# Softmax scaling of the selected-block attention moved from VectorE to GpSimd

## The reference

```python
# compressed branch: 225 overlapping 4x4 blocks, each turned into one key and one value by an MLP
attn_cmp = softmax(einsum('bhnd,bhmd->bhnm', q_c, kch) * SCALE)          # 4 heads, 1024 x 225
# selected branch: the 16 blocks with the largest summed attn_cmp, 16 tokens each = 256 keys
_, idx = top_k(attn_cmp.sum(axis=1).mean(axis=1), 16)
attn_slc = softmax(einsum('bhnd,bhmd->bhnm', q_s, ksh) * SCALE)          # 4 heads, 1024 x 256
out_slc = einsum('bhnm,bhmd->bhnd', attn_slc, vsh) @ proj_slc_w + proj_slc_b
# window branch: 25 windows of 7x7 with a relative bias
out = g[0] * out_cmp + g[1] * out_slc + g[2] * out_win
x = x + out
# then, per token: layer norm, router, layer norm, 2 of 8 experts (gelu MLP 128 -> 512 -> 128)
```

## Time and profile before

| | |
|---|---|
| median of 3 executions | 891.06 us (890.48 to 892.27) |
| span of the profiled execution | 921.8 us |
| TensorE busy | 716.2 us, 78% |
| VectorE busy | 593.9 us, 64% |
| ScalarE busy | 414.4 us, 45% |
| GpSimd busy | 240.6 us, 26% |
| first and last scaling (L897) | at 76.8 and 678.7 us |
| mean granted TensorE clock | 0.890 |

### The profile page before, as it was taken

How to read it: one execution, slowest core, us unless ns; L and a number is a source line. 1 busy time by engine, 2 the same in 40 slices (tenths; PEclk the granted TensorE clock), 3 DMA queues, 4 the chain that set the end, 5 groups by cost and what they waited for, 6 DMA issues and landing times.

```text
span 921.8 us, 18341 instructions
## 1 busy us (share of the span) xinstructions
PE 716.2 (78%) x4992; PEld 534.2 (58%) x4993; DVE 593.9 (64%) x1930; ACT 414.4 (45%) x1203; POOL 240.6 (26%) x399
## 2 busy tenths in 40 slices
PE   3998778799578788976778799577873089999963
PEld 2794444679244455964444588244452079999962
DVE  4647858788377778856869787477767234444434
ACT  2227327324353453326427333453531158887852
POOL 5000220210604002124220210604001635555540
PEclk9999969899888799989979999978885589999995
DMA  9600000000100000000000000101002212222236
GB/s 324 194 1 0 4 3 0 25 23 1 48 1 4 1 23 1 24 20 29 3 3 0 2 24 1 47 1 28 1 1 114 70 49 64 69 63 64 62 93 235
DMA packets 34225, 39.66 MB, mean 43 GB/s; under 512 B 11246, under 2 KB 26720, under 8 KB 33888
## 3 DMA queue, kind: packets, MB, share of 16 engines
q1 hardware_dynamic: 28592, 27.73, 9.9%
q0 software_dynamic: 4416, 9.00, 2.9%
q10 hardware_dynamic: 1152, 2.10, 0.6%
HBM read 25.38 MB, written 14.50 MB: 43 GB/s over the span
## 4 chain that ended last, share of the span: by engine, by line
PE 44%; issue 24%; DVE 18%; POOL 4%; DMA 3%; ACT 2%; another core or an unknown queue 2%; POOLq 1%; SPq 1%; DVEq 0%; ACTq 0%
PE ps L1579 7%; PE ps L1563 7%; PE ps L1330 6%; PE ps L1479 6%; PE ps L1353 4%; PE ps L1278 3%; PE ps L1321 2%; DVE r_P L897 2%; DVE r_kp L1096 2%; PE ps L1297 2%; PE ps L1272 2%; DVE nmx L887 2%; POOL xs_d L607 2%; DMA kbdw<-z_d 1%
## 5 line engine op out<-in xcount | busy, mean ns | idle before, releaser
L1353 PE MATMUL ps<-kbd,qT 128*128 128x450 f32 (+1 forms) x256 | 131.6, 653 | 16.2 <-issue 15.1
L668 ACT ACTIVATE r_P<-ps,nmx 128x225 f32<-128x225 f32 (+1 forms) x192 | 85.8, 461 | 91.1 <-DVE nmx L887 90.5
L887 DVE TENSOR_REDUCE nmx<-ps 128x4 f32<-128x900 f32 (+1 forms) x64 | 74.0, 1157 | 80.4 <-PE ps L1353 61.1
L804 ACT ACTIVATE R<-ps,R 128x128 f32<-128x128 f32 x292 | 83.3, 368 | 46.0 <-PE ps L1563 44.7
L1353 PEld LDWEIGHTS ps<-kbd,qT 128*128 128x128 f32 x256 | 52.2, 221 | 69.1 <-issue 66.8
L607 POOL DMA_INDIRECT xs_d<-pay,pos x64 | 62.2, 972 | 102.9 <-DVE pos L1077 84.6
L643 POOL DMA_INDIRECT z_d<-R x72 | 69.4, 964 | 67.3 <-DVE R L1243 53.2
L552 POOL TENSOR_TENSOR rstd<-vpe,minus_half 128x8 f32<-128x8 f32 x12 | 19.8, 1651 | 251.9 <-DVE vpe L862 251.9
L1272 PE MATMUL ps<-ident,r_P 128*128 128x128 f32 (+1 forms) x384 | 57.7, 297 | 34.8 <-DVE r_P L897 22.2
L1272 PEld LDWEIGHTS ps<-ident,r_P 128*128 128x128 f32 (+1 forms) x384 | 47.1, 157 | 60.1 <-DVE r_P L897 35.7
L1563 PE MATMUL ps<-R 128*128 128x128 f32 x584 | 79.3, 280 | 0.0
(11 more groups left out here) (208 smaller groups left out, 1388.2 us busy)
## 6 DMA issues: line engine op xcount, KB each, us to landing
R<-xs_d SPq DMA_DIRECT2D x76, 65.0 KB
kbdw<-z_d SPq DMA_DIRECT2D x8, 512.0 KB, 5.5
x_sb<-x SPq DMA_DIRECT2D x4, 512.0 KB, 3.5
w1k_sb<-w1k SPq DMA_DIRECT2D x1, 2048.0 KB, 10.2
w1v_sb<-w1v SPq DMA_DIRECT2D x1, 2048.0 KB, 14.6
fw_sb<-fw SPq DMA_DIRECT2D x1, 2048.0 KB, 10.5
fw_sb<-fw SPq DMA_DIRECT2D x4, 512.0 KB, 11.0
t_d<-r_P SPq DMA_DIRECT2D x4, 512.0 KB, 2.6
```

Of the source, the lines that this page charges most:

```text
L668: last = sc.activation(Pb[t % NRING][:, h, 0:m], bank(ph, name)[:, (h % 2) * m:(h % 2) * m + m], ACT.Exp, bias=nmx[:, t % NRING, h:h + 1], ...
L804: last = sc.activation(hT[:, r % 2, c, :], hid(r)[:, C * c:C * c + C], ACT.Gelu, bias=wx[:, r, O_B1 + c:O_B1 + c + 1])
L887: ve.tensor_reduce(nmx[:, t % NRING, :].rearrange("p (a h) -> p a h", a=2), v.rearrange("p a (h m) -> p a h m", h=2), AX.X, ALU.max, negat ...
L1353: mm(bank(ph, name)[:, 0:2 * mk], qT[:, 128 * t:128 * t + 128], kbd[:, 2 * k:2 * k + 2, 0:mk], start=True, stop=True).then_inc(full_sem(ph ...
```

## The change

In the selected branch (`s == "s"`) VectorE only makes the reciprocals and signals `rz_ready`. The scaling is made on GpSimd by a new function, `scale_selected`, which issues one product of 128 x 1024 elements for each tile, with the four reciprocals of a token broadcast over 256 keys each, and then signals `prob_ready`. It stands behind `windows(b)` and ahead of `head` in GpSimd's program. The wait for `dve_done` between reciprocal and scaling falls away in this branch (8 links fewer for an image). The compressed branch stays as it is.

```diff
-    LINKS_FIRST, LINKS_MIDDLE = 7, 67
+    LINKS_FIRST, LINKS_MIDDLE = 7, 59
...
+        rz_ready = sem("rz_ready")
...
+            def scale_selected(b):
+
+                for t in range(NT):
+                    pool.wait_ge(rz_ready, b * NT + t + 1)
+                    v = Pb[t % NRING][:, :, 0:256]
+                    gp.tensor_tensor(v, v, rZ[:, t % NRING, :].unsqueeze(2).to_broadcast([128, HEADS, 256]),
+                                     ALU.mult).then_inc(prob_ready, 1)
...
                 windows(b)
+                scale_selected(b)
                 head(middle_one(b), b + 1, 3 * b + 1)
...
             windows(B - 1)
+            scale_selected(B - 1)
...
                     dve.wait_ge(*copied(ph, f"S{s}{t}b"))
+                    if s == "s":
+                        ve.reciprocal(rZ[:, t % NRING, :], Z[:, t % NRING, :]).then_inc(rz_ready, 1)
+                        return
                     link(ve.reciprocal(rZ[:, t % NRING, :], Z[:, t % NRING, :]))
```

## The result

The changed kernel takes 898.55 us (median of 4 runs, 898.04 to 899.08), the kernel before, timed beside it, 890.93 us (890.48 to 892.27). By the medians it is 7.6 us slower, where +8.8 us was forecast. The ratio is 1.0069 with a 95% interval of 1.0041 to 1.0097, which is 6.1 us (3.7 to 8.6); it isn't the quotient of the two medians (1.0086), but its interval holds that too.

What follows compares the result with a forecast made beforehand. VectorE was taken to bound the selected stage at 2.98 us a tile; the longer latency loop then adds 2.2 us an image, 4 x 2.2 = +8.8 us on 891.06, giving 899.9 us, range 891 to 907 us.

Steps and rivals of the forecast that it cites:

- What bounds before: First stage of the selected branch: VectorE sets the pace, 2.98 us a tile; the latency loop's 2.73 us is hidden.
- The product: GpSimd's scaling product of 128 x 1024: 1.925 us, from a line through two other shapes.
- The loop: Latency loop over two tiles in the selected stage, through the scaling: 5.45 us becomes 6.29, 3.15 us a tile.
- the prediction's formula: TensorE's transposes in the selected stage: each of two turns from T(0) to T(4) takes 4.37 + d us.
- The walk: Event by event through the first selected stage: T(0) 0.84 us later, T(4) 2.0, the stage's end 2.2.
- The rival of the relief: Selected stage: taking scalings off VectorE wins if the product is short; -1.0 us an image, 887 us, chance 0.09.
- lower bound: GpSimd's product at the copy's rate, 1.05 us: T(4) 0.6 us earlier, -1.0 us for an image.
- The sum: Selected stage 2.2 us longer in each of four images: +8.8 us, from 891.06 to 899.9 us.
- the rival priced at up to 1 us an image: Selected stage: product takes 2.20 us (904.7 us), or more TensorE idling lowers the clock (909 us); chance 0.15.
- Hidden: The selected stage's delay is swallowed, or unprofiled runs have another critical step: 890 to 893 us, chance 0.07.
- What is free: GpSimd's eight waits in the selected stage delay nothing in its queue, and no DMA is added.
- The carried difference: The median of the runs lies 30.7 us below the profiled span of 921.8 us; carried over unchanged.

Runs made afterwards that it cites:

- e12: Kernel before with one more step between scores and transposes in the selected branch and O0 moved to step 7; 909.47 us, ratio 0.9892.
- e2: Changed kernel, but GpSimd scales heads 0 and 1, VectorE heads 2 and 3 in the plain form; TensorE waits for both; 907.64 us, ratio 1.0208.
- e3: Changed kernel, but GpSimd scales three heads and VectorE one in the plain form; TensorE waits for both; 910.66 us, ratio 1.0206.
- e4_half_left_out: Changed kernel with GpSimd scaling only heads 0 and 1, heads 2 and 3 left unscaled; 882.48 us, ratio 0.9893.
- e11_three_heads_accum: Same as e3, but VectorE scales its one head in the form that also writes a sum; 924.47 us, ratio 1.0040.
- e1: Changed kernel without any scaling in the selected branch; VectorE's reciprocal releases TensorE directly; 876.95 us, ratio 0.9820.
- e5: Changed kernel with one more step between scores and transposes in the selected branch and a fourth buffer of probabilities; 911.24 us, ratio 1.0194.
- before again: Kernel before, unchanged, run for a second profile of an ordinary execution; median 891.98 us, ratio 0.9997.
- first profile: Profiled execution of the kernel before, unchanged, that the prediction read; span 921.8 us.
- e7: Same as e2, but VectorE scales its two heads in the form that also writes a sum; 889.11 us, ratio 0.9955.
- The last four kernels: Four follow-up kernels: three with an extra step and O0 moved to step 7, one the three-head split in summing form; 908.44 to 924.47 us.

## Why the prediction was right

**What bounds before.** Confirmed: with a fourth tile in flight and VectorE's scalings kept (e12) the distance stays at 2.99 us; VectorE was the bound and not the loop.

**The product.** 1.892 us for 1.925 (x32, 1892 to 1894 ns). The line through two other shapes was right to 2%. With the products of e2 and e3 it is 1039, 1466 and 1892 ns for 512, 768 and 1024 elements: 1.67 ns an element and 0.19 us fixed. A piece of 256 elements is hardly cheaper than one of 49 (1.67 against 1.714 ns an element). That is 2.0 cycles at 1.2 GHz; the Trainium skill's figure of about 2.6, "GPSIMD Engine Reference", section 3.1, is above it, and the rows were the better source.

**The loop.** By the prediction's formula two turns, T(0) to T(4), take 2 x (4.37 + d) for a product of d us:

| product us | kernel | formula | measured |
|---|---|---|---|
| 1.041 | e4_half_left_out | 10.82 | 10.81 |
| 1.468 | e11_three_heads_accum | 11.68 | 11.66 |
| 1.892 | changed kernel | 12.52 | 12.50 |

The slope is that of latency: each microsecond on the product is one on the turn. The line ends just below e4. Without any product (e1, image 2) T(0) to T(4) still takes 10.83 us, since its first turn takes 5.65; its second, T(2) to T(4), takes 5.18 us, TensorE's own pace, against 5.40 in e4, 5.83 in e11 and 6.25 in the changed kernel, where the formula says 5.41, 5.84 and 6.26. The middle of e5 is the other side of the proof: the same product, only the step added, and no delay once a third tile spans the turn. VectorE's scalings that stand explain e2 and e3 but not the changed kernel, where VectorE has no scaling beside the product.

**The walk.** In image 2 the shifts are 0.80, 1.60, 1.87 and 2.13 us where 0.84, 1.7, 2.0 and 2.2 were forecast; nearly all of the rest is the 0.03 us that the product is shorter, up to four times over. In the first stage, where the walk was made, it is 0.53 us at T(0) and 1.55 at O1's start. One step was misread there: the walk lets T(7) start at 163.44 before the change, behind the last scaling, but T(6) ran at the low clock until then and the first matmul of T(7), the ninth of the 16 in that row, starts at 163.82 in that trace. The walk's own shift for that stage would have been 1.8 us.

The rival of the relief was priced right only up to T(7). With e4's product of 1.04 us T(4) comes 0.69 us earlier and T(7) 1.05 in image 2, where its lower bound said 0.6 and 1.0. But it made that 4 us in all, 887 us, and e4 is 9.3 us faster: its stages are 2.6 us shorter an image, since T(7) and O1 take 1.09 and 1.93 us there, against 1.59 and 2.69 in "before again".

**The sum.** +8.8 us became +7.6 by the medians, +6.1 by the ratio. Up to O1's start it is +8.6, by image 1.55, 3.17, 1.64, 2.25. Image 1 is above 2.2 because T(0) is already 1.60 us later there: the scores ahead of it took 8.32 us where they take 6.77 in "before again". The term that was off is the one I set to nothing in the forecast: the clock at the end of the stage. It acts already ahead of O1. T(7) in image 2, in "before again" and then in the changed kernel (us, busy times, and the granted clock as the third number from the end):

```profile
490.00:492.00 2.00, 1.59 (x8) 1.19 (x8) 1.27 (x2) 0.77 (x2) 0.00 (x0) 0.64 0.00 0
```
```profile
496.00:498.00 2.00, 1.31 (x16) 0.99 (x20) 0.69 (x1) 0.99 (x2) 0.00 (x0) 1.00 0.00 0
```

T(7) takes 1.59 us at 0.64 and 1.09 at 1.00, so the 2.13 us at its start are 1.64 at O1's. In "before again" O1 takes 1.93, 2.72, 2.69 and 3.64 us in the four images, after the change 3.64 in image 0 (granted clock 0.51, second window above), 2.47 in image 1 and 1.93 in images 2 and 3. What the rival priced at up to 1 us an image, more idle time ahead of T(6) and T(7), can be seen in image 0: O1 takes 1.7 us more there. In the other three it takes 0.3, 0.8 and 1.7 us less, and over the four 1.0 us comes back. Nothing here forecasts where the low stretches fall, so I call this part luck.

**Hidden.** Fell: no wait swallowed a part of the delay. Where less arrives at O1's start than at T(7)'s, in image 2, it is T(7)'s own clock. **What is free.** The compressed branch takes 122.5 us in sum in both kernels, and the stretch between the branches 122.8 and 122.5.

**The carried difference.** The 30.7 us between span and median had nothing to do with the stage, whose sum is 126.8 us in that first profile and 126.7 in "before again". In the first profile the compressed branch took 29.3, 39.5, 36.3 and 42.1 us in the four images, in "before again" 29.3, 30.0, 30.6 and 32.5.

## What to carry to other kernels

Before moving work off a busy engine, write down the loop that passes through the moved step: its latency over the number of tiles it spans is the pace that is left when the engine is free, and here (4.37 + 1.89)/2 = 3.13 us was more than the engine's 2.98. If the loop is the bound, a shorter step helps (e7, 2.6 to 4 us here) and one more tile in flight hides it whole; then move every later consumer by the same step, or the pipeline stalls at the first one left behind. Two engines that scale the same tile "in parallel" must first be shown to run side by side in a timeline.

## What was unexpected in the hardware

A plain scaling on VectorE stood for about as long as GpSimd's product ran: 349 ns alone, 1658 ns beside a product of 1466 ns, 1.49 us for two beside 1.04 us. In its form with a sum, 478 ns, it did not, nor did the copy of 128x512 out of PSUM (0.66 us at 144.60, beside the product from 144.77) or the maxima at 145.97 (1.23 us).

In five of the profiles VectorE stands still for 4 to 8 us at a time inside the compressed branch. In the first profile of before, VectorE in image 1, and the windows view there:

```profile
255.08 1.10 DVE L887 TENSOR_REDUCE nmx<-ps 128x4 f32<-128x900 f32 x1 [8.04 <-remote]
```
```profile
249.00:259.00 10.00, 2.60 (x10) 1.87 (x11) 3.89 (x10) 2.41 (x10) 2.96 (x4) 0.77 0.08 27
```

TensorE is busy for 2.60 of 10 us and stands for 7.0 us up to 257.43, ScalarE for 8.2 us up to 256.21; GpSimd works at its indirect stores until 252.66. The last four kernels, on the chip where before takes 919.9 us, show it too: the compressed branch takes 145 to 149 us in sum there, 121 to 125 in all the others but the first profile (147). What holds the engines is open; the change did not touch it.
